# Four residual layers on one core: the weight sums of each seven-product step formed by VectorE instead of GpSimd, and one pair of rank rows split earlier

## The reference, cut to what matters

```
gate = x @ W_gate.T + SCALE * (x @ A_gate[b].T) @ B_gate[b].T
up   = x @ W_up.T   + SCALE * (x @ A_up[b].T)   @ B_up[b].T
act  = silu(gate) * up
out  = x + act @ W_down.T + SCALE * (act @ A_down[b].T) @ B_down[b].T
```

## Time and profile before

| | |
|---|---|
| time, median of 3 runs | 301.48 us (301.19 to 302.86) |
| the profiled execution's own time | 302.27 us |
| its span in the profile | 300.5 us |
| PE busy | 289.2 us, 96% |
| DVE busy | 197.8 us, 66% |
| ACT busy | 143.9 us, 48% |
| POOL busy | 45.6 us, 15% |
| granted TensorE clock, each slice | nine tenths or more of full speed |

### The profile page before, as it was taken

How to read it: one execution, slowest core, us unless ns; L and a number is a source line. 1 busy time by engine, 2 the same in 40 slices (tenths; PEclk the granted TensorE clock), 3 DMA queues, 4 the chain that set the end, 5 groups by cost and what they waited for, 6 DMA issues and landing times.

```text
span 300.5 us, 4571 instructions
## 1 busy us (share of the span) xinstructions
PE 289.2 (96%) x1624; PEld 236.8 (79%) x1624; DVE 197.8 (66%) x343; ACT 143.9 (48%) x255; POOL 45.6 (15%) x67
## 2 busy tenths in 40 slices
PE   6989999999999999979999999999999999999995
PEld 5456788888888778857788888888889888888884
DVE  1287999794746999888785786776756959242003
ACT  2366862521525269665746646656634874211000
POOL 1000000000714504342143033223000000000000
PEclk9999999999999999999999999999999999999999
DMA  5979993007603000170250340420275200022004
GB/s 158 352 285 314 400 345 109 3 0 222 199 0 90 9 3 0 35 226 20 85 194 2 122 159 0 137 76 9 64 293 168 67 0 0 0 72 70 0 2 140
DMA packets 23255, 33.29 MB, mean 111 GB/s; under 512 B 2624, under 2 KB 15424, under 8 KB 23104
## 3 DMA queue, kind: packets, MB, share of 16 engines
q1 hardware_dynamic: 22944, 32.47, 32.7%
q10 hardware_dynamic: 288, 0.52, 0.5%
HBM read 30.89 MB, written 2.10 MB: 110 GB/s over the span
## 4 chain that ended last, share of the span: by engine, by line
PE 72%; DVE 11%; SPq 5%; DMA 4%; ACT 4%; issue 3%; ACTq 0%; DVEq 0%
PE bank L1225 11%; PE bank L1226 11%; PE bank L1227 11%; PE bank L1348 8%; PE bank L1349 8%; PE bank L1350 8%; DMA w_raw<-in_w 3%; SPq L383 3%; PE bank L1330 2%; DVE bgu_st L965 2%; PE bank L1198 2%; PE bank L1180 2%; PE bank L1473 2%; SPq L439 2%; DVE wc_up L791 1%
## 5 line engine op out<-in xcount | busy, mean ns | idle before, releaser
L534 ACT ACTIVATE part<-bank 128x512 f32<-128x512 f32 x44 | 26.0, 594 | 30.3 <-PE bank L1350 30.3
L1225 PE MATMUL bank<-act_hl,wd_hl 128*128 128x512 f32 (+1 forms) x99 | 36.5, 369 | 0.0
L1226 PE MATMUL bank<-act_hl,wd_hl 128*128 128x512 f32 (+1 forms) x99 | 36.3, 367 | 0.0
L1227 PE MATMUL bank<-act_hl,wd_hl 128*128 128x512 f32 (+1 forms) x99 | 36.2, 366 | 0.0
L1040 DVE TENSOR_TENSOR part<-bank,part 128x512 f32<-128x512 f32 x44 | 29.1, 681 | 6.7 <-PE bank L1330 6.6
L791 DVE TENSOR_TENSOR w_hl<-w_raw,w_hl 128x512 fp32r<-128x512 f32 x29 | 19.0, 687 | 11.4 <-ACT w_hl L534 11.4
L965 DVE SCALAR_TENSOR_TENSOR bgu_st<-bgu_st,lo_rows,bgu_raw 128x512 fp32r<-128x512 f32 x22 | 18.3, 866 | 11.4 <-ACT bgu_st L534 11.3
L534 ACT ACTIVATE act_hl<-act_f 128x512 fp32r<-128x512 f32 x22 | 13.6, 624 | 20.8 <-PE bank L1227 18.8
L534 ACT ACTIVATE w_hl<-w_raw 128x512 fp32r<-128x512 f32 x29 | 17.7, 625 | 12.2 <-DMA w_raw<-in_w 12.1
L791 DVE TENSOR_TENSOR act_hl<-act_f,act_hl 128x512 fp32r<-128x512 f32 x22 | 14.9, 687 | 12.9 <-ACT act_hl L534 12.8
L516 POOL TENSOR_TENSOR s_tmp<-wgu_raw 128x256 f32<-128x256 f32 x11 | 8.4, 764 | 84.1 <-DVE wc_up L791 41.9
(11 more groups left out here) (162 smaller groups left out, 698.3 us busy)
## 6 DMA issues: line engine op xcount, KB each, us to landing
w_raw<-in_w SPq DMA_DIRECT2D x22, 256.0 KB, 7.5
wgu_raw<-in_wgu SPq DMA_DIRECT2D x11, 512.0 KB, 4.4
bgu_raw<-in_bgu SPq DMA_DIRECT2D x40, 128.0 KB, 2.7
w_raw<-in_w SPq DMA_DIRECT2D x7, 512.0 KB, 7.3
wd_raw<-in_wd SPq DMA_DIRECT2D x4, 704.0 KB, 5.9
out<-x_f SPq DMA_DIRECT2D x7, 256.0 KB, 2.4
x_f<-in_xT SPq DMA_DIRECT2D x6, 256.0 KB, 7.4
w_raw<-in_w SPq DMA_DIRECT2D x1, 1024.0 KB, 6.5
```

What stands on the lines that cost most here:

```text
L534: return act.activation(dst, src, ACT.Copy)
L1225: pe.matmul(dst, w_hi, x[0][:, cols], start=start, stop=False)
L1226: pe.matmul(dst, w_hi, x[1][:, cols], start=False, stop=False)
L1227: return pe.matmul(dst, w_lo, x[0][:, cols], start=False, stop=stop)
```

## The change

POOL's `form_s` is gone. DVE has it as `form_s(n, k)`, one sum at a time, called in the order 0, 2, 1, 3. In steps 0 and 1 the four stand together, for step 2 they stand before `wc_low(2, 0)`, and from step 3 on they are spread over the loop: sums 0 and 2 at the head of the iteration, 1 and 3 around `wc_low(n+1, 0)`. POOL clears `td_st` as soon as the second rank spread of layer 3 is done. `bgu_low(1, 0..1)` moves ahead of `t3_low(1)` on DVE, and `add_c(0, 0)` behind both. On PE `p3(1)` moves ahead of `lora_y(0)`.

```diff
@@ gpsimd @@
-            def form_s(n):
...
-            for n in range(STEPS):
-                form_s(n)
-                if n == 2:
-                    pool.wait_ge(t3_done, H)
-                    pool.memset(td_st[:].bitcast(F32), 0.0).then_inc(td_zeroed, 1)
+            pool.wait_ge(t3_done, H)
+            pool.memset(td_st[:].bitcast(F32), 0.0).then_inc(td_zeroed, 1)
@@ vector @@
+            def form_s(n, k):
+
+                (a11, a12), (a21, a22) = ((wgu_block(n, i, 0, 2), wgu_block(n, i, 2, C)) for i in range(2))
+                if k == 0:
+                    for fc, _ in rows_of(n):
+                        dve.wait_ge(wgu_in[raw_slot(fc)], 16 * raw_uses(fc))
+                    if n == 0:
+                        dve.wait_ge(l2_tm, H)
+                    else:
+                        dve.wait_ge(wc_lo, 3 * n - 1)
+                    ins = dve.tensor_tensor(s_tmp[:, 0], a21, a22, ALU.add)
+                elif k == 1:
+                    dve.wait_ge(s_formed, 4 * n + 1)
+                    ins = dve.tensor_tensor(s_tmp[:, 1], s_tmp[:, 0], a11, ALU.subtract)
+                elif k == 2:
+                    ins = dve.tensor_tensor(s_tmp[:, 2], a11, a21, ALU.subtract)
+                else:
+                    dve.wait_ge(s_formed, 4 * n + 3)
+                    ins = dve.tensor_tensor(s_tmp[:, 3], a12, s_tmp[:, 1], ALU.subtract)
+                ins.then_inc(s_formed, 1)
+
@@ vector @@
             t2_uv_low(1)
+            for k in (0, 2, 1, 3):
+                form_s(0, k)
             wc_low(0, 0)
...
             bgu_low(0, 0)
+            for k in (0, 2, 1, 3):
+                form_s(1, k)
             x_add(2, 1, 0)
@@ vector @@
             xt_low(3)
-            t3_low(1)
-            add_c(0, 0)
             for i in range(2):
                 bgu_low(1, i)
-            for k in range(1, 4):
+            t3_low(1)
+            for k in range(4):
                 add_c(0, k)
+            for k in (0, 2, 1, 3):
+                form_s(2, k)
             wc_low(2, 0)
@@ vector @@
             for n in range(2, STEPS):
                 p, g = divmod(n, 2)
                 more = n + 1 < STEPS
+                if more:
+                    form_s(n + 1, 0)
+                    form_s(n + 1, 2)
                 for k in (2, 3):
                     add_c(n - 1, k)
                 if more:
+                    form_s(n + 1, 1)
                     wc_low(n + 1, 0)
+                    form_s(n + 1, 3)
@@ tensor @@
             p6(1)
+            p3(1)
             lora_y(0)
             p4(0)
             lora_z_x(0)
-            p3(1)
             p7(1)
```

## The result

The changed kernel takes 303.58 us (median of 22 runs, 302.10 to 305.21), the one before 302.38 in the 22 runs made beside it: a ratio of 1.0038, with a 95% interval of 1.0020 to 1.0055. (One of those 22 took 1637.1 us and is not in the ratio.) That is 1.15 us slower: clear of noise, but within the 0.5% that the forecast took for the noise of a comparison. The forecast gave 0.50 to "slower" by more than that and 0.40 to "the same", which is what came. Forecast were 303.4 and +1.89 us, on a median of 301.48 that three runs had given and that more runs put 0.9 higher.

What follows compares the result with a forecast made beforehand. PE, 96% busy, was taken to bound the kernel, so DVE and POOL act only through PE's waits. +1.11 through step 3 and +0.78 in steps 5, 7, 9 gave +1.89 on 301.48: 303.4 us, range 300.4 to 304.8.

Steps and rivals of the forecast that it cites:

- Prices: DVE's cost per sum: 418 ns, 0.34 us of queue with overlap; four standing together 1.54 us.
- Steps 0 and 1: form_s(0) costs nothing in DVE idle time; form_s(1) makes PE late by a net 0.11 us.
- The rank rows: Layer 3's second rank-row transfers: SP issues them from 121.3 instead of 124.66 us, ending the stall's old cause.
- DVE late next: DVE's queue into step 2: bgu_low(2,0) starts at 133.78 us, so lora_w(2) wins only 0.2 of 2.3 us.
- the bound for being wrong: Sign against the forecast: bgu_low(2,0) on DVE starting by 133.0 us.
- Steps 5, 7, 9: Copies that p6 waits for come 0.45 us late; PE loses 0.26 three times, +0.78 us.
- Even steps: All of form_s(5) fits DVE's 1.33 us idle ahead of wc_low(5,1) with 0.10 relief: cost 0.
- lag nothing: Rank-row transfers of steps 4 to 10 start with the splits and cause no delay; no cost given.
- the forecast's own case: The main forecast, +1.89 us to 303.4 us, own range 302.7 to 304.3; chance 48%.
- the stall goes: Rival: DVE reaches bgu_low(2,0) by 132.4 us, PE saves 2.3 at lora_w(2); 300.0 or 299.2 us; 10%.
- balance: Rival: form_s(3)'s end and the odd steps' copies are early enough; +0.3 to +0.8, 301.8 to 302.3 us; 36%.
- the dearer sums: Rival: sums on DVE cost 0.42 us each with no overlap, 1.8 us more, 305.1 us; 6%.

Runs made afterwards that it cites:

- e3: The changed kernel with sums 0 and 2 behind, not ahead of, the two add_c in the loop from step 2 on; ratio 0.9999.
- e7: The changed kernel with one extra 128x256 sum on DVE ahead of the two add_c in steps 3, 5, 7 and 9; ratio 1.0069.
- e9: e8 with step 3's four sums right behind step 2's rank splits, and add_c(2,1) ahead of wc_low(3,1); 300.48 us, ratio 0.9943.
- e2: The changed kernel with the old order on DVE and PE put back, all sums still on DVE; ratio 1.0022.
- e8: The changed kernel with the edits of both e3 and e4; ratio 1.0014.
- e4: The changed kernel with bgu_low(2,0..1) ahead of add_c(1,1) and act_product(0,1) on DVE; ratio 1.0048.
- e1: The kernel before with only the change's new order on DVE and PE, the sums staying on POOL; ratio 1.0033.
- e6: The changed kernel with p3(1) put back behind lora_z_x(0) on PE; ratio 1.0041.

## Why the prediction was right, point by point

- **Prices.** The sums took 418 to 420 ns (0.418 forecast), a group 1.46 us (1.54): the wait for the one just before costs 0.11 here, not 0.18. Given back at `wc_low(1,0)` and `bgu_low(0,0)`: the pair takes 1.26 us (96.84 to 98.10) instead of 2.28, so 1.02; 1.00 was forecast, and 1.5 by the prediction's reading of the Trainium skill. The lock that the Trainium skill describes ("SBUF — State Buffer", who interferes with whom) can still be what acts, if the VectorE instruction waits only for what is left of the GpSimd one; that is argued and not tested, and my reading of a whole 0.76 each was the wrong one.
- **Steps 0 and 1.** `lora_w(1)` is 0.1 late, as forecast.
- **The rank rows.** Issued 3.5 earlier (3.4 forecast), no ACT wait for them at step 2.
- **DVE late next.** `bgu_low(2,0)` starts at 132.13, which is 29.40 behind `thin3(0)`: 29.56 was forecast (133.78), and the bound for being wrong (133.0) is 28.78, since layer 3 begins 1.49 earlier in this profile. `lora_w(2)` 0.39 earlier; 0.2 was forecast. `p7(2)`'s new wait: there, and `lora_z(2)` 0.40 late where 0.6 was forecast. Step 3 begins 0.47 late (0.66), leaves `p6(3)` 0.86 late (1.11). These three differ by some 0.2: DVE was 0.16 early at `bgu_low(2,0)`, half of it the cheaper group of sums, and the rest is 0.01 or 0.02 in each instruction behind it.
- **Steps 5, 7, 9.** 0.28, 0.29 and 0.28 (0.26 forecast), e3 and e7 show the cause from both sides.
- **Even steps.** No wait, as forecast: from `lora_y(3)` to `lora_y(5)` only step 5's 0.28 is added.
- **Read wrongly: "lag nothing" of the later transfers.** In the kernel before ACT waited 0.34 us for rank rows in step 6 (at 174.66) and 0.62 in step 8 (at 196.07). It cost PE nothing there, nor does a wait of 0.70 in step 8 of e9, and the kernel after has none; but in e2 PE lost 0.3 us behind such a wait (0.66) and in e8 0.6 (1.33). So there was a slack here that could run out, and the prediction gave it no price.
- **What was off is the step from the stretch to the time.** The stretch says +1.69, the times say +1.15 (0.6 to 1.7 by the interval). The sum assumed that a wait of PE costs its own length, in both kernels alike. In the kernel before it often seems to cost more, below; that this is the missing half microsecond was only argued.
- **The time itself was met by luck.** 303.4 was forecast and 303.58 came, because a median before that was 0.9 too low and a step that was 0.7 too large nearly cancel. And +0.38% is under the 0.5% that the forecast's own case was to exceed.

Of the rivals, *the stall goes* was wrong for the reason given (e4: the stall goes and the time doesn't); *balance* describes the verdict on the time, +0.38%, but not its cause (its slacks were not there: PE lost 0.28 in each of steps 5, 7 and 9); the dearer sums did not occur.

## What to carry to other kernels

Moving work onto an engine that is 66% busy is not paid by its share but by its place: ahead of the instruction for which another engine's queue waits, with no slack left, a 0.33 us sum cost PE 0.33 us in each of four steps (e7), and behind two instructions of the same queue, where that queue waited 0.89 us anyway, two sums cost nothing (e3). When a late transfer is cured, look at once at what else stood behind the same wait, since a second queue may have been ready only just in time. And an order that fits one placement of work can be wrong for another: e1's order loses with the sums on POOL and costs nothing with the sums on DVE.

## What the runs showed of the hardware that was not expected

**A wait of PE can cost more than its length.** In e1, e4 and e8 the granted clock falls from 2.4 to 1.2 GHz (1.00 to 0.50 in the windows above) when PE has just begun to work again (0.1 to 0.7 us before) after an idle time of its weight loads of 2.1 to 2.6 us, and stays there for some 3.4 us. Over e8's windows the shares missing add up to 1.7 us of full-speed work; at `lora_y(3)` 0.87 of it is left against e3, since waits behind the fall became shorter. After the same 2.59 us at `lora_w(2)` as in e1, the profiled run of the kernel before kept its full clock (PE began again at 134.81):

```profile
135.00:136.00 1.00, 1.00 (x6) 0.88 (x6) 1.00 (x2) 0.16 (x1) 0.35 (x1) 1.00 0.47 193
```

Its other runs often did not: of the 31 beside e1 to e4, 21 report a mean clock of 0.994 or less, with a median span of 300.5 us, and 10 a full one, with 299.5. Of the 25 beside e6 to e9 it was 9, with 300.4 against 300.25, so the price is not settled by them. Of the 22 runs of the kernel after, whose longest wait is 2.10 and not 2.59, it was 2; so the change may give something back here that its stretch at full clock does not show. That would be in line with the missing half microsecond: at full clock alone the median spans are 301.7 after (20 runs) against 299.5 and 300.25 before, 1.5 to 2.2 apart, but these were not run side by side. The longest wait alone does not decide it: 7 of 10 runs of e1 (2.59) are at 0.994 or less, 2 of 10 of e2 (2.30) and 3 of 10 of e6 (1.68). e3's ten runs report 0.997 or more, e9's 0.998 or more in six of seven.

In which place the clock of those runs fell no profile shows. Open is also why with a wait of 2.1 us it is 0.994 or less in 11 of the 20 runs of e4 and e8, where it stands at `p7(2)` behind another of 0.7, and the 2.10 at `lora_w(2)` of the kernel after in 2 of 22, the 2.09 there in none of e3's 10.
